# One-hot matrices built from 16-bit columns with the edge index innermost, and ranks by 13 broadcast matrix products a group

## The reference, cut to what matters

```python
h = relu(layernorm(x)); x = x + GIN(h)          # two sums over edges: segment_sum(h[src], dst), each with an MLP
h = relu(layernorm(x)); x = x + attention(h)    # scores per edge, softmax over the edges of a dst, sum per dst
h = relu(layernorm(x)); x = x + tent_conv(h)    # msg = sum_k basis_k(edge) * (h[dst] @ w_k), summed per src
h = relu(layernorm(x)); x = x + spline_conv(h)  # B-spline corners (8 per edge) of h[dst] @ W_k, mean per src
# the positions of the last layer come from a smaller net on the same graph (stn1 .. stn4):
new_pseudo = clip(pseudo + t[dst] - t[src], 0, 1)
```

## Time and profile before

| what | us |
|---|---|
| median of three runs | 10376.03 |
| the profiled execution | 10374.36 |
| its span in the profile | 10372.6 |
| DVE busy | 6788.9 (65%) |
| POOL busy | 7124.9 (69%) |
| PE busy | 5565.9 (54%) |
| ACT busy | 2942.8 (28%) |

### The profile page before, as it was taken

How to read it: one execution, slowest core, us unless ns; L and a number is a source line. 1 busy time by engine, 2 the same in 40 slices (tenths; PEclk the granted TensorE clock), 3 DMA queues, 4 the chain that set the end, 5 groups by cost and what they waited for, 6 DMA issues and landing times. The chain is left out here.

```text
span 10372.6 us, 152846 instructions
## 1 busy us (share of the span) xinstructions
PE 5565.9 (54%) x36304; PEld 4649.1 (45%) x36433; DVE 6788.9 (65%) x16516; ACT 2942.8 (28%) x7350; POOL 7124.9 (69%) x10729
## 2 busy tenths in 40 slices
PE   4333255554666665767674666666544444753333
PEld 3333244443544443455553666666434444433332
DVE  6555477775522222688887888888567777656666
ACT  0000022221144442122222777777421111410000
POOL 3888788885088885688884555555158888058887
PEclk8555556555577775666665555555565555865555
DMA  6332222221666764233334999999332223888887
GB/s 205 124 123 78 63 67 70 69 68 54 184 247 249 252 247 119 66 82 85 82 82 136 351 352 353 355 352 351 113 98 50 48 47 45 321 288 236 236 236 207
DMA packets 894626, 1760.55 MB, mean 170 GB/s; under 512 B 486978, under 2 KB 487287, under 8 KB 889896
## 3 DMA queue, kind: packets, MB, share of 16 engines
q0 software_dynamic: 317952, 1023.05, 31.5%
q1 hardware_dynamic: 537384, 598.27, 17.3%
q10 hardware_dynamic: 39168, 138.04, 3.4%
HBM read 1150.36 MB, written 611.50 MB: 170 GB/s over the span
## 5 line engine op out<-in xcount | busy, mean ns | idle before, releaser
L1694 POOL DMA_INDIRECT got<-corners,now x1664 | 1700.9, 1022 | 1399.7 <-DVE now L1682 645.3
L1694 POOL DMA_INDIRECT got<-node_rows,now x1664 | 1683.1, 1011 | 733.1 <-issue 666.4
L146 POOL MEMSET spare<- 128x192 f32 x4944 | 1377.0, 279 | 2.7
L1694 POOL DMA_INDIRECT got<-patches,now x832 | 810.5, 974 | 442.1 <-DVE now L1682 281.2
L2464 PE MATMUL sum_p<-msg_s,hot_s 128*128 128x64 f32 x3328 | 734.2, 422 | 509.3 <-DVE msg_s L1942 509.3
L2464 PEld LDWEIGHTS sum_p<-msg_s,hot_s 128*128 128x128 f32 x3328 | 717.7, 332 | 515.2 <-issue 515.2
L893 POOL DMA_INDIRECT d_rows<-row x832 | 820.5, 986 | 184.1 <-issue 150.5
L647 POOL DMA_INDIRECT s_rows<-row_now,pos_i x784 | 758.3, 967 | 158.2 <-issue 129.6
L2020 PE MATMUL acc_p<-msg,hot_s 128*128 128x32 f32 x1664 | 376.2, 402 | 797.7 <-DVE msg L1950 797.7
L2020 PEld LDWEIGHTS acc_p<-msg,hot_s 128*128 128x128 f32 x1664 | 362.7, 330 | 812.0 <-issue 812.0
L1739 DVE TENSOR_TENSOR a<-a,sum_p 128x64 f32 x832 | 183.9, 221 | 822.4 <-issue 357.5
(11 more groups left out here) (417 smaller groups left out, 14281.7 us busy)
## 6 DMA issues: line engine op xcount, KB each, us to landing
corners<-z SPq DMA_DIRECT2D x245, 960.0 KB
corners<-z SPq DMA_DIRECT2D x98, 864.0 KB
d_rows<-empty ACTq DMA_DIRECT2D x32, 1586.0 KB
row<-d_rows SPq DMA_DIRECT2D x104, 488.0 KB
corners<-z SPq DMA_DIRECT2D x49, 672.0 KB
s_rows<-empty ACTq DMA_DIRECT2D x32, 962.0 KB
row<-s_rows SPq DMA_DIRECT2D x104, 296.0 KB
got<-node_rows,now POOLq DMA_INDIRECT x1664
```

The source lines that it names most:

```text
L146: pool.memset(self.of[:, t, :], 0.0).then_inc(self.cleared, 1)
L1694: pool.indirect_dma_start(out=to[b][:, t, :], out_offset=None, in_=table, in_offset=bass.IndirectOffsetOnAxis(ap=indices.now[b][:, t:t + 1 ...
```

## The change

- `one_hot` now compares 16-bit numbers, with the tile index (eight edges of a partition) innermost: output `[LO, LO, T]` bf16, a full `column16` of `[LO, LO, T]` (each number eight times), and `lo` as eight 16-bit values that repeat for each of the 128 nodes.
- `column16` is filled at each phase's start: by one DVE copy of 1024 elements in SBUF in the turning phase, both sums and the score phase (`fill_columns`), and in PSUM in the tent and spline phases by eight DVE instructions and eight PE transposes (`PsumColumns`).
- `lo` is kept in bf16: `k.lo_d` (written by ACT in the first sum) and a new `k.lo_s` (written by DVE in the turning phase, ahead of the one-hot; ACT's copy to `k.head_s` goes). The first sum copies `lo` to a small tile `lo_now` ahead of the one-hot.
- PE takes the one-hot of a tile as `hot[:, :, t]`: its stationary operand is read at a step of eight elements, 16 bytes. ACT's widening copy reads `hot16` at that step and writes `hot_s` as before.
- The spline phase makes a bf16 one-hot and has ACT widen it; PE now waits for ACT there.
- `place_phase`: each product with ones is done once for all the tiles behind it, with the moving operand repeated; the total is a fifth part of the second bank of `rank_p`.

```diff
+def fill_columns(k, dve, c, column16):
+    c.after(dve.tensor_copy(column16[:], last(k.column[:], T)))
+class PsumColumns:
+    def __init__(self, k, ph):
+        self.rows = sb(k, ph, "rows", [LO, T, LO], BF16)
+        self.of = pb(k, ph, "column16", [LO, LO, T], BF16)
+    def begin(self, dve):
+        for j in range(T):
+            m = dve.tensor_scalar(self.rows[:, j, :], self.k.ones16[:], self.k.eighth[:], float(j * (LO // T)), ALU.mult, ALU.add)
+        m.then_inc(self.rowed, 1)
+        dve.wait_ge(self.columned, 1)
+    def turn(self, pe):
+        flat = self.of[:].rearrange("p l t -> p (l t)")
+        pe.wait_ge(self.rowed, 1)
+        for j in range(T):
+            m = self.k.nc.tensor.transpose(flat[:, j * LO:(j + 1) * LO], self.rows[:, j, :], self.k.ident16[:])
+        m.then_inc(self.columned, 1)
-def one_hot(k, dve, out, lo, column=None):
-    return dve.tensor_tensor(out, mid(k.column[:] if column is None else column, T), last(lo, LO), ALU.is_equal)
+def one_hot(dve, out, column16, lo):
+    return dve.tensor_tensor(out, column16, mid(lo, LO), ALU.is_equal)
# place_phase, PE, for each group
-                        for t in range(T):
-                            to = rank_p[b][0:P, t // 4, (t % 4) * 2 * KEYS:(t % 4 + 1) * 2 * KEYS]
-                            nc.tensor.matmul(to, before16[:], one[:, t, :], start=True, stop=t == 0)
-                            for u in range(t):
-                                nc.tensor.matmul(to, k.ones16[:], one[:, u, :], start=False, stop=u == t - 1)
-                        for u in range(T):
-                            m = nc.tensor.matmul(total_p[b][:, 0:2 * KEYS], k.ones16[:], one[:, u, :],
-                                                 start=u == 0, stop=u == T - 1)
+                        nc.tensor.matmul(upon(0, 0, 4), before16[:], one[:, 0:4, :], start=True, stop=False)
+                        for u in range(3):
+                            nc.tensor.matmul(upon(0, u + 1, 3 - u), k.ones16[:], mid(one[:, u, :], 3 - u), start=False, stop=u == 2)
+                        nc.tensor.matmul(upon(1, 4, 5), k.ones16[:], mid(one[:, 0, :], 5), start=True, stop=False)
+                        nc.tensor.matmul(upon(1, 4, 4), before16[:], one[:, 4:8, :], start=False, stop=False)
+                        for u in range(1, T):
+                            first = max(4, u + 1)
+                            m = nc.tensor.matmul(upon(1, first, T + 1 - first), k.ones16[:], mid(one[:, u, :], T + 1 - first),
+                                                 start=False, stop=u == T - 1)
# turn_phase
-                        one_hot(k, dve, hot16[b2][:], row[b][:, :, SLO], column_p).then_inc(hot, 1)
+                        c.after(dve.tensor_copy(k.lo_s[:, tiles(g)], row[b][:, :, SLO]))
+                        one_hot(dve, hot16[b2][:], column16[:], k.lo_s[:, tiles(g)]).then_inc(hot, 1)
-                            m = nc.tensor.transpose(turned_p[:, t, :], hot16[b2][:, t, :], k.ident16[:])
+                            m = nc.tensor.transpose(turned_p[:, t, :], hot16[b2][:, :, t], k.ident16[:])
-                        nc.scalar.copy(hot_s[b % 2][:], hot16[b % 2][:]).then_inc(widened, 1)
+                        nc.scalar.copy(hot_s[b % 2][:], hot16[b % 2][:].rearrange("p l t -> p t l")).then_inc(widened, 1)
-                        nc.scalar.copy(k.head_s[:, tiles(g), SLO], row[b][:, :, SLO])
# first_sum_phase
-                        one_hot(k, dve, hot_d[b % 2][:], row[b][:, :, DLO]).then_inc(hot, 1)
+                        c.after(dve.tensor_copy(lo_now[b % 2][:], row[b][:, :, DLO]))
+                        one_hot(dve, hot_d[b % 2][:], column16[:], lo_now[b % 2][:]).then_inc(hot, 1)
# second_sum_phase and score_phase: fill_columns ahead of indices.first, one_hot and hot_d[:, :, t] likewise
# tent_phase
-                dve.tensor_copy(column_p, k.column[:])
+                column.begin(dve)
                 cells(dve, c, 0)
-                        one_hot(k, dve, hot16[b2][:], k.head_s[:, tiles(g), SLO], column_p).then_inc(hot, 1)
+                        one_hot(dve, hot16[b2][:], column.of[:], k.lo_s[:, tiles(g)]).then_inc(hot, 1)
# spline_phase
-                        one_hot(k, dve, hot_s[b2][:], k.head_s[:, tiles(g), SLO], column_p).then_inc(hot, 1)
+                        one_hot(dve, hot16[b2][:], column.of[:], k.lo_s[:, tiles(g)]).then_inc(hot, 1)
+                        act.wait_ge(hot, g + 1)
+                        nc.scalar.copy(hot_s[b % 2][:], hot16[b % 2][:].rearrange("p l t -> p t l")).then_inc(widened, 1)
-                        pe.wait_ge(hot, g + 1)
+                        pe.wait_ge(widened, g + 1)
```

More of the change, by code:

```diff
@@ L559, in _ @@
                             s.run[0:P, :].unsqueeze(1).unsqueeze(1).broadcast_to([P, 2, 4, 2 * KEYS]), ALU.add))
-                        dve.tensor_tensor(s.run[:], s.run[:], total_p[b][:, 0:2 * KEYS], ALU.add)
+                        dve.tensor_tensor(s.run[:], s.run[:], rank_p[b][:, 1, 4 * 2 * KEYS:5 * 2 * KEYS], ALU.add)
                         c.after(dve.tensor_tensor(at(rank_p, b), at(rank_p, b), s.one[b][:].rearrange("p (c t) h -> p c t h", c=2), ALU.mult))
@@ L925, in _ @@
             def _(dve):
+                c = Chain(dve, own)
+                fill_columns(k, dve, c, column16)
                 with dve.Fori(0, QUADS) as i:
+                    c.again()
                     for b in range(4):
@@ L1704, in second_sum_phase @@
     with phase(nc) as ph:
+        column16 = columns(k, ph)
         got = [sb(k, ph, "got", [LO, T, 3 * D_HID], BF16) for _ in range(4)]
-        hot_d = [sb(k, ph, "hot_d", [LO, T, LO], BF16) for _ in range(2)]
+        hot_d = [sb(k, ph, "hot_d", [LO, LO, T], BF16) for _ in range(2)]
         sum_p = [pb(k, ph, f"sum_p{b}", [LO, T, D_HID]) for b in range(2)]
@@ L1887, in _ @@
                         nc.scalar.copy(turned_s[:], turned_p[:]).then_inc(copied, 1)
-                        nc.scalar.copy(hot_s[b][:], hot16[b][:]).then_inc(widened, 1)
+                        nc.scalar.copy(hot_s[b][:], hot16[b][:].rearrange("p l t -> p t l")).then_inc(widened, 1)
             @block.tensor
             def _(pe):
+                column.turn(pe)
                 clear_sums(k, acc_p, 4).then_inc(summed, 1)
@@ L1960, in spline_phase @@
         hot_s = [sb(k, ph, "hot_s", [LO, T, LO]) for _ in range(2)]
+        hot16 = [sb(k, ph, "hot16", [LO, LO, T], BF16) for _ in range(2)]
         acc_p = pb(k, ph, "acc_p", [LO, 4, 512])
@@ L1965, in spline_phase @@
         weight = [w[:, 0:T * 8].rearrange("p (t x) -> p t x", x=8) for w in weight_p]
-        column_p = pb(k, ph, "column_p", [LO, 512])[:, 0:LO]
-        hot, based, weighed, summed, own, seen = ph.sems("hot", "based", "weighed", "summed", "own", "seen")
+        column = PsumColumns(k, ph)
+        hot, based, weighed, widened, summed, own, seen = ph.sems("hot", "based", "weighed", "widened", "summed", "own", "seen")
         gathered = Landings(ph, "gathered", 4)
@@ L1985, in _ @@
                 indices.first(dve)
-                c.after(dve.tensor_copy(column_p, k.column[:]))
+                column.begin(dve)
                 dve.sem_inc(based, 2)
@@ L2052, in score_phase @@
     with phase(nc) as ph:
+        column16 = columns(k, ph)
         got = [sb(k, ph, "got", [LO, T, D_HID]) for _ in range(4)]
         prod = [sb(k, ph, "prod", [LO, T, D_HID]) for _ in range(4)]
-        hot_d = [sb(k, ph, "hot_d", [LO, T, LO], BF16) for _ in range(8)]
+        hot_d = [sb(k, ph, "hot_d", [LO, LO, T], BF16) for _ in range(8)]
         turned16 = [sb(k, ph, "turned16", [LO, T, LO], BF16) for _ in range(4)]
@@ L2536, in one_hots @@
                     nc.scalar.copy(lo_now[:, 0], k.lo_d[:, tiles(g)])
-                    steps.after(nc.scalar.copy(lo_now[:, 1], k.head_s[:, tiles(g), SLO]))
+                    steps.after(nc.scalar.copy(lo_now[:, 1], k.lo_s[:, tiles(g)]))
                     for t in range(T):
@@ L2715, in clear @@
             dve.memset(k.lo_d[:, G * T:], -1.0)
+            dve.memset(k.lo_s[:, G * T:], -1.0)
             dve.memset(k.src_d[:, G * T:], 0)
```

52 lines of the change are left out of this document (34 added, 18 removed).

## The result

The kernel after the change takes 10214.04 us (median; 10212.41 to 10217.0) against 10375.37 us for the kernel before, measured beside it: ratio 0.9845, 95% interval 0.9828 to 0.9862. That is 161 us less, where the forecast was 100 us less and the range ended at 10235. Its profiled execution has a span of 10215.1 us, 157.5 us less than that of before (10372.6).

What follows compares the result with a forecast made beforehand. POOL was taken to bound turning, place, second sum and spline, DVE score and tent, PE and DMA the first sum. Score −52, tent −38, second sum −21, turning +3, first sum +8 gave −100: 10276 us, range 10235 to 10400.

Steps and rivals of the forecast that it cites:

- The score phase: Score phase, bound by DVE's in-order stream: 104 one-hots each 0.54 us shorter, less small costs, −52 us (bounds −60 and +1).
- The one-hot: DVE's one-hot of 1024 elements in all six phases: 0.69 us in place of 1.225, at the 256-element cast's pace.
- Rival B: Tent phase: PSUM operands don't go two at a time, one-hot stays 1.22 us; sum −59, 10317 us; chance 0.14.
- Rival C: One-hot: two 16-bit sources gain nothing, or not with a repeated `lo`; +10 to +30, 10386 to 10406 us; chance 0.08.
- Tent: Tent phase: DVE's quad falls to 44.9 us and meets POOL's 45.1; phase 1192 to 1199 us, −38 (bounds −48, +3).
- Second sum: Second sum: shorter one-hots delay POOL's indirect DMAs less, 33 us become 11; −21 us with the column's fill (bounds −33, +1).
- Turning: Turning phase: one-hot with two SBUF inputs mostly misses POOL's DMA starts, +2, and longer column fill, +1; bounds 0 and 52 us.
- First sum: First sum: PE's 24 products read weights at a 16-byte step, 50 to 79 ns each; +8 us with the column's fill.
- rival A's full form: First sum: stepped weight load takes a product from 50 to about 110 ns, +150 us there; about 10438 us; chance 0.15.
- ACT's widening: ACT's widening copy at the 16-byte step: 1.05 us becomes 1.7 us, once a group of 11 us, covered.
- Place: Place phase: 13 products stream the same 4400 columns as 44 did, and DVE waits for scatters anyway; 0 us.
- spline: Spline phase: POOL alone bounds it, and the added hop over ACT is two groups ahead of need; 0 us.

Runs made afterwards that it cites:

- fills alone: Kernel before with 30 one-column fills of an unused tile appended to DVE's stream at the end of the place phase: 10310.13 us, ratio 0.9935.
- the runs with 100 and 200 fills: Kernel after with 100 or 200 one-column fills of an unused tile at the end of DVE's place-phase stream: 10259.46 us and 10254.82 us.
- the run with lo_d in fp32: Kernel before with the 16-bit one-hot in the score phase alone, lo_d left an fp32 tile: 10383.64 us, ratio 1.0005.
- the run with the column in PSUM: Kernel after with the turning phase's old one-hot back (fp32 column in PSUM) and the second sum's 16-bit column in PSUM: 10201.98 us, ratio 0.983.
- its own experiment: Kernel after with the place phase's 44 products a group of before (total_p back): 10217.32 us, ratio 0.9845.

## Why the prediction was right or wrong

**The score phase, the step that failed.** The prediction said that DVE has "only the short gaps between dependent steps and the loop's turns beside" its busy time, and took the turns as something that stays. They were 3.6 + 2.0 us, twelve times, and it neither priced them nor asked what they are. The list of waits shows them under "issue". The change added 20 DVE instructions ahead of the loop, and that moved it. 57 of the 61 us by which the forecast missed are this (1354.4 to 1296.9 by fills alone). It was luck that the move went the right way: the runs with 100 and 200 fills show what other places cost. The one-hot's own part, forecast at −52, is −56 with the stall away and −40 to −50 with it.

**The one-hot.** 0.69 us from the cast of 256 elements: measured 689 to 694 ns. Rival B is out: of the 312 one-hots above, the 104 of the tent and the 104 of the spline phase read their column from PSUM, at 691 and 684 ns. The Trainium skill (VectorE: DVE Perf Modes, the perf-mode tier table) puts tensor_tensor with any PSUM operand at 1×; the trace does not agree, 0.691 us for 1024 elements where the earlier trace rows has 1.224 before, and the measurement decides. Rival C is out for this change, but the run with lo_d in fp32 shows its place: 1.25 us.

**Tent:** −45 for −38. 1192.6 us is the low end of the forecast of 1192 to 1199. POOL bounds it now: before, it paused for more than 1 us 17 times in the phase, most of them 1.86 us, 29 us in all; after, once, 1.25 us. The DMA mean fell by 9 ns, 8 us in all, which the forecast had not counted; the rest is the lag of DVE behind POOL at the end. The −38 rested on the one-hot's 0.69 us with its column in PSUM, and that held.

**Second sum:** −18 for −21, its DMAs at 963 ns where 0.97 us was given. The estimate by the square of the length left 11 of 33 us. Against the 953 ns of the run with the column in PSUM, 832 × (995 − 953) ns = 35 us became 832 × (963 − 953) ns = 8 us.

**Turning:** +14 for +3, the right mechanism with the wrong size. I reasoned from one spot, where the one-hot begins 0.28 us after a DMA does, and forecast a run from 0.53 to 1.22 us, mostly a miss. After the change the one-hot of the timeline above begins 1.01 us after the DMA ahead of it (1809.35) and covers the next start. Of 832 DMAs 102 are late, against 11 before. The 102 lie 13.7 us in all above 0.985 us each (the 11 before: 0.9), which is the phase's loss: 10.1 us in 62 that began under a one-hot, and 3.7 us in 40 that began under a small product of the spline basis (L858, L861: 120 elements, both inputs in SBUF), which the prediction had not considered. What moved the one-hot by these tenths is not shown. A relation in time read at one place was too little to rest a term on; the bound of 52 us held, and the term should have stood between.

**First sum:** 0 for +8. The price per product was read too high before (50 ns, in truth at most 31), and for the step the forecast kept to the bound of 1.57, where it is 2.0. That 62 ns lies within its bound of 79 is luck: the two errors partly cancel. Only rival A's full form, at chance 0.15, had such a ratio (110 / 50), and from its too high price it had +150 us. That nothing is lost is as the prediction allowed, PE's pause hides it: a group's 24 products take 1.21 us before and 1.64 after. Both stay below the 2.1 us at which rows arrive, and PE's pause shrank from 0.73 to 0.30 us:

```profile
2663.95 1.64 PE L1004 MATMUL acc_p<-row,hot_d 128*128 128x32 bf16 x24 [0.30 <-issue]
```

**ACT's widening** at the step: forecast 1.7 us, measured 2.03 (mean of the 104 in the turning phase, 1.05 before), covered as said. **Place** and **spline:** 0, as forecast, place by its own experiment. **Message:** −4 us; in all runs it takes 1746.5 to 1752.0 us whatever was changed, so this is scatter.

**The sum.** With the turn's stall priced, −100 would have been −157, and the profiled executions differ by 157.5. The 57 were measured afterwards, so this closes the account and is no forecast. The small misses (turning +11, first sum −8, tent −7, second sum +3, the rest about 0) nearly cancel, which is luck.

## What to carry to other kernels

Read the waits for "issue" at a loop's turn before costing anything else. If they are microseconds and not tenths, and the instruction queue has packets at every turn, then an edit that adds or removes instructions of that engine ahead of the loop can gain or lose them. Some harmless instructions are a cure to try first. A comparison between two kernels should check this before it credits the edit. For the one-hot itself: every operand in 16 bits, down to the smallest, and one of the two inputs in PSUM where GpSimd issues indirect DMAs; put the strided read where an engine has time, since it doubles a weight load and a copy of ACT.

## What the runs showed of the hardware that I had not expected

- DVE's code comes in packets of 8.2 KB. A loop of 335 instructions ran without fetches from places 1014, 1024, 1025 and 1154 of its stream and with five packets a turn from 994, 995, 1114 and 1214; there the turn was 3.7 to 5.9 us longer than the other intervals, and 0.5 to 0.6 us without fetches.
- The short one-hot is had also with one input in PSUM (691 ns for 1024 elements), and is lost with one fp32 source of eight elements a partition (1247 ns).
- A stationary operand at a step of 16 bytes takes TensorE 62 ns a product of 32 columns, at most 31 ns without. ScalarE's copy of 1024 elements from bf16 to fp32 takes 2.03 us with such a step and 1.05 without.
- An indirect DMA of POOL that begins at least 0.045 us after a one-hot with both inputs in SBUF, and over 0.25 us before its end, ends 0.82 to 0.86 us after that one-hot (133 of 133 late). With one input in PSUM none of 87 was late, and with either none that began before its one-hot.
